# Routed rows scattered one at a time, and the second image's patch loads all begun by SyncE

## The reference, cut to what matters

```python
x = x + conv_block(layernorm_over_channels(x))     # four dilated branches (1, 4, 8, 12)
t = tokens(x)                                      # 2 * 9216 tokens of 256 values
t = t + moe(layernorm(t))                          # 8 experts, each token goes to its best 2
```

## Time and profile before

| | |
|---|---|
| median of three runs | 2258.05 us |
| the profiled execution's span | 2561.4 us |
| PE busy | 2032.5 us (79%) |
| DVE, ACT, POOL busy | 1571.4, 1336.8, 1102.4 us |
| granted TensorE clock, mean | 0.863 |
| DMA | 459.86 MB, mean 180 GB/s |

### The profile page before, as it was taken

The page is one execution under the profiler, slowest core; times in us unless marked ns, Lnnn a source line. Parts: engine busy times, 40 slices in busy tenths (PEclk is TensorE's granted clock), DMA queues, the critical chain, the costliest instruction groups (busy, mean ns, idle before and its releaser), DMA issues.

```text
span 2561.4 us, 56574 instructions
## 1 busy us (share of the span) xinstructions
PE 2032.5 (79%) x20204; PEld 1920.6 (75%) x20204; DVE 1571.4 (61%) x4176; ACT 1336.8 (52%) x2869; POOL 1102.4 (43%) x1466
## 2 busy tenths in 40 slices
PE   5798899999699798878777776766676758988853
PEld 5788899999699787777777766666675657888842
DVE  5667665666577566546555554665665646766765
ACT  4576443333477545444444426665564637777732
POOL 4567122322276513433444442455655554444420
PEclk9899899999899888888787887887876869999975
DMA  5642455676443265556566567554554436777879
GB/s 172 220 127 76 140 157 144 166 174 172 119 142 111 81 192 176 161 163 170 183 181 182 157 213 237 164 171 154 174 174 152 152 121 228 252 257 255 276 267 369
DMA packets 340865, 459.86 MB, mean 180 GB/s; under 512 B 82749, under 2 KB 261437, under 8 KB 338237
## 3 DMA queue, kind: packets, MB, share of 16 engines
q1 hardware_dynamic: 229696, 245.14, 33.8%
q10 hardware_dynamic: 68433, 109.55, 12.8%
q0 software_dynamic: 42464, 101.56, 11.6%
HBM read 291.86 MB, written 174.69 MB: 182 GB/s over the span
## 4 chain that ended last, share of the span: by engine, by line
PE 47%; ACT 16%; another core or an unknown queue 9%; issue 8%; DVE 7%; DMA 6%; POOL 3%; ACTq 3%; SPq 1%; POOLq 1%; DVEq 0%
PE ps_y L426 15%; PE ps L426 7%; PE ps_a L426 6%; PE ps_o L1064 6%; PE ps_b L1001 4%; ACT e_act L1468 3%; ACT w_now L1479 3%; DMA o_acc<-res_scratch 2%; POOL taps L2147 2%; ACT h_hi L1471 1%; PE ps_tok L895 1%; PE ps_o L1051 1%; PE ps_k L846 1%; PE ps_a L939 1%
## 5 line engine op out<-in xcount | busy, mean ns | idle before, releaser
L426 PE MATMUL ps_y<-cat_hi,wp 128*128 128x288 f32 x2048 | 504.4, 322 | 10.9 <-issue 9.0
L2205 POOL DMA_INDIRECT expert_out<-e_out,e_dest x320 | 327.7, 1024 | 414.0 <-DVE e_out L2027 350.2
L2183 POOL DMA_DIRECT2D patches<-rows_scratch x348 | 194.7, 603 | 609.9 <-PE ps_o L1051 405.8
L426 PEld LDWEIGHTS ps_y<-cat_hi,wp 128*128 128x128 f32 x2048 | 370.6, 203 | 17.9 <-issue 15.9
L2127 POOL DMA_INDIRECT expert_in<-r_ln,r_pos x288 | 286.1, 993 | 114.0 <-issue 86.2
L2147 POOL TENSOR_TENSOR taps<-taps,g_rows 96x108 f32<-96x108 f32 (+3 forms) x440 | 259.9, 617 | 166.5 <-ACT g_rows L1303 162.6
L426 PE MATMUL ps<-w,h_hi 128*128 x1280 | 271.5, 309 | 75.7 <-DVE h_lo L2016 47.4
L1941 DVE SCALAR_TENSOR_TENSOR cat_lo<-ps_o,cat_hi 128x288 fp32r<-128x288 f32 (+1 forms) x576 | 228.0, 419 | 161.0 <-ACT cat_hi L1423 131.2
L426 PE MATMUL ps_y<-cat_lo,wp 128*128 128x288 f32 x1024 | 317.3, 310 | 6.3 <-issue 6.2
L1417 ACT ACTIVATE bands<-ps_b 112x288 f16<-112x288 f32 (+4 forms) x256 | 105.1, 411 | 406.3 <-PE ps_b L1001 325.9
L426 PE MATMUL ps<-e_hi,w_now 128*128 128x256 f32 x1280 | 283.9, 303 | 26.2 <-issue 21.3
(11 more groups left out here) (202 smaller groups left out, 4656.6 us busy)
## 6 DMA issues: line engine op xcount, KB each, us to landing
e_x<-expert_in SPq DMA_DIRECT2D x160, 260.0 KB
patches<-rows_scratch SPq DMA_DIRECT2D x160, 192.0 KB
patches<-rows_scratch SPq DMA_DIRECT2D x256, 108.0 KB
patches<-rows_scratch SPq DMA_DIRECT2D x192, 112.0 KB
x_in<-in_x SPq DMA_DIRECT2D x48, 384.0 KB, 3.6
rows_scratch<-rows_st SPq DMA_DIRECT2D x48, 384.0 KB, 4.3
r_x<-in_x ACTq DMA_DIRECT2D x72, 256.0 KB
r_y<-y_scratch ACTq DMA_DIRECT2D x72, 256.0 KB
```

Source lines behind the costliest of these rows:

```text
L426: mm = eng.matmul(out, lhs[p], rhs[q], start=start and n == 0, stop=stop and n == 2)
L2183: pool.dma_start(patch_target(s, n), patch_source(m, s, n)).then_inc(patch_pooled[s % RING], 16)
L2205: pool.indirect_dma_start(out=ys_dram, out_offset=bass.IndirectOffsetOnAxis(ap=e_dest[:, i, j:j + 1], axis=0), in_=e_out[:, u, j], in_offs ...
```

## The change

It does three things.

1. In the second convolution (`m == 1`) SP begins all patch loads; `second_queue` has the image as a further argument and is false for image 1. The counts that PE waits for (`loaded`) follow. The first convolution is as before.
2. In the second convolution the scatters of a pair are begun one by one. Scatter k of pair p waits until unit `placed(p) + 1 + 3k // 2` is counted in `out_ready`. The waits for `r_placed` (first scatter of the pair) and `r_lnd` (now per tile) stay.
3. In the expert stream a scatter of a pair comes behind a single indirect DMA of `send`, spread over 8 to 9 half tiles (`2 * (placed(p) // 4 - 1) + 4k // 5`) in place of three tiles with four behind each.

The number of DMAs, their sizes, sources and targets are the same.

```diff
-        def second_queue(s, n):
+        def second_queue(m, s, n):
-            return n % 2 == 1 if kind(s) == 3 else kind(s) == 0 and n >= 6
+            return m == 0 and (n % 2 == 1 if kind(s) == 3 else kind(s) == 0 and n >= 6)
...
-            def scatter_rows(p, q):
-                if q == 0:
+            def scatter_row(p, k):
+                t, z = divmod(k, TOP)
+                if k == 0:
                     pool.wait_ge(r_placed, p + 1)
-                    pool.wait_ge(r_lnd, TP * (p + 1))
-                for k in range(4 * q, 4 * q + 4):
-                    t, z = divmod(k, TOP)
-                    pool.indirect_dma_start(...)
+                if z == 0:
+                    pool.wait_ge(r_lnd, TP * p + t + 1)
+                pool.indirect_dma_start(...)
...
+                def scatter_unit(i):
+                    p, k = divmod(i, ROWS_OUT)
+                    return plans[0].placed(p) + 1 + 3 * k // 2
+                def paced_scatters(sent, before_unit):
+                    while sent < CPAIRS * ROWS_OUT and scatter_unit(sent) < before_unit:
+                        pool.wait_ge(out_ready, m * UNITS + min(scatter_unit(sent), UNITS))
+                        scatter_row(*divmod(sent, ROWS_OUT))
+                        sent += 1
+                    return sent
...
-            def scatter_after(p, q):
-                return plans[1].placed(p) // 4 - 1 + q
+            def scatter_half(i):
+                p, k = divmod(i, ROWS_OUT)
+                return 2 * (plans[1].placed(p) // 4 - 1) + 4 * k // 5
+            for n in range(STREAM):
                 for j in range(S // 128):
+                    send(n, j)
+                    while sent < CPAIRS * ROWS_OUT and scatter_half(sent) <= 2 * n + j:
+                        p, k = divmod(sent, ROWS_OUT)
+                        scatter_row(CPAIRS + p, k)
+                        sent += 1
```

More of the change, by code:

```diff
@@ L68 @@
 XROWS = IMAGES * XBLOCK
+ROWS_OUT = TP * TOP
 EARLY = 5
@@ L592, in loaded @@
         def loaded(m, s, second):
-            count = lambda k: sum(second_queue(k, n) == second for n in range(loads(k)))
-            upto = sum(count(k) for k in range(s % RING, s + 1, RING))
-            return 16 * (upto + m * sum(count(k) for k in range(s % RING, STEPS, RING)))
-        def second_queue(s, n):
-            return n % 2 == 1 if kind(s) == 3 else kind(s) == 0 and n >= 6
+            count = lambda i, k: sum(second_queue(i, k, n) == second for n in range(loads(k)))
+            upto = sum(count(m, k) for k in range(s % RING, s + 1, RING))
+            return 16 * (upto + sum(count(0, k) for k in range(s % RING, STEPS, RING) if m))
+        def second_queue(m, s, n):
+            return m == 0 and (n % 2 == 1 if kind(s) == 3 else kind(s) == 0 and n >= 6)
         def patch_source(m, s, n):
@@ L2172, in _ @@
                 enter(pool, m * (2 * N_ENG) + 2 * N_ENG)
-                def scatter_step(p, q):
-                    return step_of_tick[plans[0].placed(p)] + 3 + q
-                thirds = 0
+                def scatter_unit(i):
[7 more added lines that the diff above has]
+                    return sent
+                sent = 0
                 for s in range(1, STEPS):
-                    shared = [n for n in range(loads(s)) if second_queue(s, n)]
+                    shared = [n for n in range(loads(s)) if second_queue(m, s, n)]
+                    free_at = unit(s - RING + 1) if s >= RING else 0
+                    if m:
+                        sent = paced_scatters(sent, free_at)
                     if shared and s >= RING:
-                        pool.wait_ge(out_ready, m * UNITS + unit(s - RING + 1))
+                        pool.wait_ge(out_ready, m * UNITS + free_at)
                     for n in shared:
                         pool.dma_start(patch_target(s, n), patch_source(m, s, n)).then_inc(patch_pooled[s % RING], 16)
-                    while m and thirds < 3 * CPAIRS and scatter_step(thirds // 3, thirds % 3) <= s:
-                        scatter_rows(thirds // 3, thirds % 3)
-                        thirds += 1
                 if not m:
                     leave(pool)
-            while thirds < 3 * CPAIRS:
-                scatter_rows(thirds // 3, thirds % 3)
-                thirds += 1
+            sent = paced_scatters(sent, 2 * UNITS)
+            assert sent == CPAIRS * ROWS_OUT
             pool.wait_ge(y_added, 4 * IMAGES * Y_UNITS)
```

26 lines of the change are left out of this document (11 added, 15 removed).

## The result

The changed kernel takes 2333.07 us (median of four runs, 2319.48 to 2337.08), the kernel before 2258.24 (four runs, 2256.24 to 2268.76). The ratio is 1.031, interval 1.0272 to 1.0348: 75 us slower. My forecast was 2256 (2212 to 2292), no change. Both the size and the sign were wrong, and "slower" had 0.28.

The account below looks back on a forecast made before the run. Without stalls, PE was taken to bound the second convolution and POOL's scatters the stream's first 80 tiles. Scatters 0, stream 0, SP +3 and up to +2, less a few us of stalls: net -2, 2256 us (2212 to 2292).

Parts of the forecast that it names:

- The 303 us put down to the profiled execution: Whole kernel: profiled 2561.4 us against 2258.05 timed; the excess stalls were taken as absent from timed runs.
- The sum that closed to 35 us: Whole kernel: stage times rebuilt without stalls gave 2223 us, leaving 35 us of the timed median for stalls and waits.
- The term reasoned from POOL: Stream's first 80 tiles: 4.29 scatters of 1.27 us, 5.44 us per tile while pairs come, 414 us in all.
- Scatters one by one, second convolution: Second convolution: spacing the scatters returns nothing in timed runs, up to 205 us in the profiled execution.
- Scatters one by one, stream: Expert stream: POOL's 343 us stand and only the order changes; 0, bounds -8 to +8 us.
- rival C: Stream: a scatter comes too late for ACT's buffer, 1 to 3 us for each of nine pairs, 2272 us; chance 0.05.
- Rival D: Stream: scatters stay back to back since POOL has no idle time; costs and gives nothing; no separate chance.
- The last scatter two tiles later, covered by 21 us: Stream, handover of image 1: last scatter 11 us later, with 21 us of cover before the fill lands; cost 0.
- All patch loads on SP: Second convolution: SP begins all patch loads, at most 20.8 us per class; +3 us, at most 61.
- Short by 0.2 us per class, 3 us over 16: Second convolution, kind 3: 18 loads land after 14.3 us, PE needs them at 14.1; 3 us over 16 classes.
- Rival B: Second convolution: SP becomes the bound, at each kind-3 step, 16 to 48 us, 2280 us (2270 to 2315); chance 0.23.
- Kind 0 cost 0 as forecast: Second convolution, kind 0: a 5.5 us step plus 0.8 routing against SP's 6.3, two steps of cover: 0.

Follow-up runs that it names:

- e0: The kernel before, unchanged, on a stalling chip (13): 2556.3 us.
- e5: The kernel before, unchanged, on a quiet chip (1): 2261.18 us.
- e8: Changed kernel with patch loads shared with POOL again and stream scatters two behind each half tile, quiet chip 3: 2262.40 us, 0.9997 of the kernel before.
- e16: Changed kernel with shared patch loads and stream scatters two behind each half tile, repeated on quiet chip 2: 2260.46 us, 1.0007 of the kernel before.
- e15: The changed kernel, unchanged, on stalling chip 7: 2428.49 us, 0.9558 of the kernel before.
- e1: Changed kernel with the stream's loop as before, so only the second convolution's part, stalling chip 13: 2455.16 us, 0.9595 of the kernel before.
- e6: Changed kernel with stream scatters two behind each half tile, each pair ending as early as before, quiet chip 1: 2290.46 us, 1.0119 of the kernel before.
- e10: Changed kernel with only the last pair's stream scatters two behind each half tile, quiet chip 3: 2323.29 us, 1.0274 of the kernel before.
- e17: Changed kernel with stream scatters two behind each half tile but three half tiles later, quiet chip 2: 2348.58 us, 1.0385 of the kernel before.
- e7: Changed kernel with the second convolution's patch loads shared with POOL as before, quiet chip 1: 2296.35 us, 1.016 of the kernel before.
- e4: The changed kernel, unchanged, on quiet chip 1: 2325.48 us, 1.028 of the kernel before.
- e9: Changed kernel with only the two kind-0 loads of each step given back to POOL, quiet chip 3: 2322.82 us, 1.0267 of the kernel before.

## Why the prediction was wrong, step by step

**The 303 us put down to the profiled execution: wrong.** It was the first choice of the prediction, and it shaped the rest. e0 shows the kernel before at 2556 to 2559 us with and without a profile, e5 at 2261 to 2263 with and without. The trace looks like that of a stalling chip, the timed runs like those of a quiet one. What I took from it, that without stalls the spacing returns nothing, holds on quiet chips all the same (e8, e16). For the execution of the trace ahead I had 2360 to 2460 us, and the changed kernel's 2428 on a chip of that kind (e15) lies in that. That is in part luck, since the forecast had only the spacing's gain and the 2428 has the two costs below in it.

**The sum that closed to 35 us closed by chance.** Against e5's 2260.4 its terms were: start 892 for 898.7; second convolution 431 for 489.1; then 34 for 43.3; first 80 tiles with the handover 414 + 19 = 433 for 423.4; 334 + 99 = 433 for 405.9. The second convolution was 58 us too low: PE is busy for 27 us more than the 372 + 50 that I had added up, at a clock of 0.94 in place of 0.99, and idle for some 30 more. The last two terms were 37 too high, most of it because rows of a stalling chip went into them. Errors of both signs made a closure that I read as proof. The term reasoned from POOL, 4.29 scatters of 1.27 us per tile, was the good one: with the handover 433 against 423 to 426.

**Scatters one by one, second convolution: 0, right here** (485.3 against 489.1). On a stalling chip it returns 110 us with SP's cost inside (e1 against e0).

**Scatters one by one, stream: 0, wrong, +37 us.** The failed step is "the r_ln buffer is asked for about two tiles (11 us) behind the last scatter, in place of four: cost 0 unless POOL lags by more". POOL does lag by more, and the same paragraph had said why: 4.29 scatters of 1.27 us need 5.44 us per tile against PE's 4.7, so work piles up in front of the scatter due last. From 1842.73 to 1891.45 us of after, POOL's timeline has nothing but scatters with 0.30 us between. This is rival C, "a scatter comes too late for ACT's buffer", with its nine pairs and its place exactly, at 5.4 us per pair (48.8 / 9) in place of 1 to 3, and with a chance of 0.05. e6 takes it away, e10 shows that it isn't the last pair, e17 brings it back with another spacing. How the wait costs time I read from the rows and didn't test: ACT's copy stands before its work on the tiles, e_out comes later, and POOL, the engine that was short of time, waits 109.0 us for it in place of 70.2. Rival D, back-to-back scatters in the stream, holds for long stretches, but it put the price at nothing, and the order alone had one.

**The last scatter two tiles later, covered by 21 us: cost 0, by luck.** The cover was the stalling chip's. On a quiet chip the chain runs from the last scatter to the handover before the change too (e5), so there was none. Ending the last pair earlier gives nothing in the median all the same (e10).

**All patch loads on SP: +3, wrong, +29 us** (e7; 32 in the second convolution of e4). SP's work was sized nearly right: 16 x 19.6 + 16 x 6.3 = 415 us, and its 616 loads in that stage sum to 426 in e4. With the stores it is 22 us per class, where I had 20.8 at the most. The failed step is "Short by 0.2 us per class, 3 us over 16". It asked only whether the 18 loads of kind 3 come in time, and only for the case that SP begins them when their buffer comes free. For kind 3 alone its numbers were close: 11.8 us to begin and 2.2 to land (medians of after) against a window of 16.2 in e5, for my 14.3 against 14.1. The 3.1 us for the landing was the wrong row, though: the 112 KB loads of the earlier trace rows are POOL's of kind 0, while those of kind 3 have 32 KB, and the page has no time for them. What I left out is that the loads of kinds 1 and 2 stand behind the 18 and take 7 us to land. By the table above SP comes to kind 1's a median of 6.7 us late, and 13 of 48 steps start late. Rival B I set aside with "every ordinary wait lengthens the class and with it SP's time". The class of the kernel before was long, (1387.8 - 1010.6) / 16 = 23.6 us on the quiet chip, and the move still cost 1.5 to 1.7 us per class (401.8 us for 16 classes after, 404.5 in e4). SP begins loads in one order; it waits for a free buffer or for ACT's residual block first (55 us in all), and is then busy for 22 of the 25 us of a class (15 of 24 before), so a wait is made good slowly. B's price of 1 to 3 us per class and its own time, 2280 (2270 to 2315), hold: e6, which has only this part's cost, takes 2290. Its place, each kind-3 step, does not. Kind 0 cost 0 as forecast (e9). "Up to 2 us at the end" is there: 43.3 to 45.7.

The Trainium skill ("DMA: Bandwidth & Descriptors", section "Issuing engines are not separate DMA queues") has the sequencer's time as usually small beside the DMA. Here the trace shows otherwise: SP needs 11.55 us to begin the 18 loads at 1037.15, and the last of such a row lands a median of 2.2 us later. Giving the nine back to POOL takes the 29 us away (e7).

**The rivals together.** B and C were both true. I had weighed them as alternatives; added to the median as I priced them they make 2258 + 22 + 14 = 2294, already outside my range, and as measured on chip 1 2258 + 29 + 35 = 2322. The result is 11 us over that. Against e4 its trace is 6 us longer, all of it in the rest (411.5 for 404.1), which no part of the change touches.

**What stays open.** Why bursts of scatters stall all engines on some chips was not found; the runs show only that spacing removes most of it in the second convolution, where POOL has time to space, and hardly any in the stream (538.9 to 571.9 us in its spaced versions, 555.3 before), where it has none. The version of e8 was not run on a stalling chip. How much of the 1.5 us per class goes to SP's time for the nine loads and how much to its fixed order, in which kind 1's loads and ACT's residual stores stand in one line with them, was not told apart: no run has another order.

## What to carry to other kernels

Where one engine sets a stage's pace, its work is already late by the end of each group. Moving the last piece of a group later then costs whoever needs the buffer, though the work is the same (here 4 us per pair for three half tiles, some 8 us). Leave the end where it is. Before loads move onto a queue, count that queue's time to begin them against the measured period, and then ask what stands behind them: the loads that the move makes late may be the next ones. Here a queue busy for 15 of 24 us made one step late, and one busy for 22 of 25 made thirteen. And when a trace and the timed runs differ by 13%, ask whether both are of the same machine before any row is used.

## What was not expected of the hardware

The same program, the kernel before, has medians of 2259 to 2262 us on three chips (37 runs, 2249 to 2272) and of 2540 and 2559 on two (15 runs, 2537 to 2565). All that comes before the second convolution, which has no scatters of routed rows, ends alike on all (891 to 899 us). The two kinds part where POOL scatters routed rows: 489 against 633 us in the second convolution, 423 against 555 in the stream's first 80 tiles. The sign of this change hangs on it: 1.026 to 1.031 on quiet chips, 0.956 on a stalling one. The granted clock goes with it, as these lines of the kernel before on chip 13 show beside those above:

```profile
893.00:1526.00 633.00, 513.58 (x6196) 478.39 (x6193) 356.10 (x1122) 273.52 (x738) 239.23 (x314) 0.82 0.61 173
1567.00:2123.00 556.00, 394.40 (x2690) 370.12 (x2691) 343.08 (x1024) 326.85 (x602) 307.30 (x298) 0.79 0.52 163
```

PE is busy 65 us longer for the same matmuls at 0.82 in place of 0.94, and idle for 119 in place of 49.
